# Loading the node features and layer weights of a graph network's first stage from GpSimd instead of SyncE, and turning both weight matrices first

## What is computed

```python
def _L0_gnn_ref(x, Ws_self, Ws_neigh, bs, src, dst):
    deg = segment_sum(ones, dst, n)
    for l in range(3):
        neigh = segment_sum(h[src], dst, n) / clip(deg, 1)
        h = h @ Ws_self[l] + neigh @ Ws_neigh[l] + bs[l]     # relu but for the last
def _mlp(x, W0, b0, W1, b1, g, b):
    return _ln(silu(x @ W0 + b0) @ W1 + b1, g, b)
def _L1_gnn_ref(...):
    e = _mlp(edge_feat, emb_W0, ...)
    e_new = _mlp(concat([e, mesh_nfeat[src], grid_nfeat[dst]]), edge_W0, ...) + e
    agg = segment_sum(e_new, dst, n)
    return _mlp(concat([grid_nfeat, agg]), node_W0, ...) + grid_nfeat
x = _ln(x + _L0_gnn_ref(x, ...)); x = _ln(x + _L1_gnn_ref(x, ...))
```

## Time and profile before

| | us |
|---|---|
| median of 3 runs (2293.87 to 2297.41) | 2294.68 |
| profiled execution | 2294.92 |
| its span from first to last instruction | 2293.2 |
| TensorE busy | 2192.8 |
| VectorE busy | 1502.4 |
| ScalarE busy | 1217.4 |
| GpSimd busy | 1209.9 |

### The profile page before, as it was taken

How to read it: one execution, slowest core, us unless ns; L and a number is a source line. 1 busy time by engine, 2 the same in 40 slices (tenths; PEclk the granted TensorE clock), 3 DMA queues, 4 the chain that set the end, 5 groups by cost and what they waited for, 6 DMA issues and landing times. The chain is left out here.

```text
span 2293.2 us, 44871 instructions
## 1 busy us (share of the span) xinstructions
PE 2192.8 (96%) x13036; PEld 1881.2 (82%) x13040; DVE 1502.4 (66%) x3372; ACT 1217.4 (53%) x2244; POOL 1209.9 (53%) x1721
## 2 busy tenths in 40 slices
PE   2989998999999999999999999999999999999898
PEld 2437886878778989989889898998989989889776
DVE  4813996353846776766766767667676676766666
ACT  1122113242337667666676766676676667667421
POOL 0387107786415555555555555555555555555223
PEclk7999999999999999999999999999999999999899
DMA  8232001010266323333332333333233333333131
GB/s 217 74 78 49 1 0 43 3 44 3 60 199 169 65 61 63 64 59 64 62 65 60 61 65 62 64 64 61 62 59 65 63 64 64 62 59 66 26 95 45
DMA packets 81519, 149.80 MB, mean 65 GB/s; under 512 B 20229, under 2 KB 20695, under 8 KB 81460
## 3 DMA queue, kind: packets, MB, share of 16 engines
q0 software_dynamic: 47248, 93.38, 21.4%
q1 hardware_dynamic: 34212, 55.67, 8.0%
HBM read 128.90 MB, written 19.71 MB: 65 GB/s over the span
## 5 line engine op out<-in xcount | busy, mean ns | idle before, releaser
L1654 ACT ACTIVATE b_bank<-c_bias 128x512 f32<-128x512 f32 x528 | 315.9, 598 | 15.1 <-PE b_bank L1766 5.2
L145 POOL DMA_INDIRECT s_attrs<-k_attrs,k_row_i x170 | 225.4, 1326 | 165.7 <-POOLq L2220 114.9
L1587 DVE CUSTOM_DVE_ANT_0 b_bank<-b_bank,c_p,k_floor 128x512 f32<-128x512 f32 x176 | 132.5, 753 | 255.7 <-PE b_bank L1788 254.8
L1432 POOL DMA_INDIRECT c_from_src<-s_dst_table,c_at_nodes x173 | 278.6, 1610 | 32.0 <-issue 32.0
L1843 PE MATMUL b_bank<-k_m_hi,c_pt_hi 128*128 128x512 f32 x704 | 293.8, 417 | 0.0
L1419 POOL DMA_INDIRECT c_from_src<-s_mesh_table,c_at_nodes x176 | 202.2, 1149 | 152.3 <-POOL c_at_nodes L1415 144.2
L1844 PE MATMUL b_bank<-k_m_lo,c_pt_hi 128*128 128x512 f32 x704 | 277.9, 395 | 0.0
L1845 PE MATMUL b_bank<-k_m_hi,c_pt_lo 128*128 128x512 f32 x704 | 274.0, 389 | 0.0
L1438 POOL TENSOR_TENSOR c_dev<-c_var,k_half 128x1 f32<-128x1 f32 x176 | 99.7, 566 | 327.1 <-DVE c_var L1569 327.1
L1725 ACT ACTIVATE c_h<-c_from_src 128x512 f32<-128x512 f32 x176 | 111.2, 632 | 263.3 <-DVE c_from_src L1608 263.3
L1786 PE MATMUL b_bank<-c_m_hi,c_ht_hi 128*128 128x384 f32 x704 | 222.5, 316 | 6.3 <-DVE c_ht_lo L1574 6.0
(11 more groups left out here) (352 smaller groups left out, 5859.8 us busy)
## 6 DMA issues: line engine op xcount, KB each, us to landing
k_w<-in_L_gnn_Ws_self_dram SPq DMA_DIRECT2D x3, 1024.0 KB, 6.8
k_w<-in_L_gnn_Ws_neigh_dram SPq DMA_DIRECT2D x3, 1024.0 KB, 10.8
c_from_src<-s_mesh_table,c_at_nodes POOLq DMA_INDIRECT x176, 3.5
c_from_src<-s_dst_table,c_at_nodes POOLq DMA_INDIRECT x173, 4.7
s_attrs<-k_attrs,k_row_i POOLq DMA_INDIRECT x170, 2.6
a_mesh<-in_L_gnn_mesh_nfeat_dram SPq DMA_DIRECT2D x10, 224.0 KB
k_h<-in_x_dram SPq DMA_DIRECT2D x1, 2240.0 KB
s_mesh_table<-a_mesh_out SPq DMA_DIRECT2D x10, 224.0 KB
```

The costliest lines, as they stand in the source:

```text
L145: return pool.indirect_dma_start(scratch["attrs"], bass.IndirectOffsetOnAxis(ap=k["row_i"][0:EP, c:c + 1], axis=0), k["attrs"][0:EP, A4 * ...
L1432: pool.indirect_dma_start(from_src[u][:], None, scratch["dst_head" if head else "dst_table"], bass.IndirectOffsetOnAxis(ap=at_nodes[u][:, ...
L1587: dve.tensor_tensor_reduce(var1_bank[:], var1_bank[:], p[u % 2][:], 1.0 / D, k["floor"][:, 0:1], ALU.mult, ALU.add, var[u][:, 0:1]).then_i ...
L1654: act.activation(bank[:], bias[:, m, :], ACT.Copy).then_inc(bank_set, 1)
```

## The change

Four edits, all in `phase_a`. The loads of the node features and of the two weights of the first layer are issued by GpSimd, after its constants and once `weights_in` is 48, and no longer by SyncE. TensorE turns both `w1` before the first product, and ScalarE copies both out first; the bias product stands right after the turning, the totals products after jobs 0 and 1. ScalarE copies the first two turned mesh tiles before, not after, `w_hi` and the first two `hc`.

```diff
@@ SyncE
-        for part in PARTS:
-            sp.dma_start(k["h"][part, :, :], t["x"].rearrange("(b p) d -> p b d", p=NPB)[part, :, :]).then_inc(next_in, 16)
-        sp.dma_start(k["w0"][:], chunked(t["L0_gnn_Ws_self"][0])).then_inc(next_in, 16)
-        sp.dma_start(k["w1"][:], chunked(t["L0_gnn_Ws_neigh"][0])).then_inc(next_in, 16)
-
@@ GpSimd
+        pool.wait_ge(weights_in, 48)
+        for part in PARTS:
+            pool.dma_start(k["h"][part, :, :], t["x"].rearrange("(b p) d -> p b d", p=NPB)[part, :, :]).then_inc(next_in, 16)
+        pool.dma_start(k["w0"][:], chunked(t["L0_gnn_Ws_self"][0])).then_inc(next_in, 16)
+        pool.dma_start(k["w1"][:], chunked(t["L0_gnn_Ws_neigh"][0])).then_inc(next_in, 16)
@@ ScalarE
-        copy_turned(0)
+        for i in range(2):
+            copy_turned(i)
         act.wait_ge(pool_const, 10)
         for j in range(NJ):
-            if j == KC:
-                copy_turned(1)
...
-        act.wait_ge(next_in, MOVED + 32)
-        for i in range(2):
-            act.activation(w_hi[i][:], w[i][:], ACT.Copy).then_inc(w_hi_ok, 1)
-
-        def copy_h(n):
-            if n >= 2:
-                act.wait_ge(hc_turned, n - 1)
-            act.activation(hc[n % 2][:], h[:, n, :], ACT.Copy).then_inc(hc_ok, 1)
-
-        for n in range(2):
-            copy_h(n)
-
...
         for u in range(2):
             mesh_copy(u, u, True)
+        act.wait_ge(next_in, MOVED + 32)
+        for i in range(2):
+            act.activation(w_hi[i][:], w[i][:], ACT.Copy).then_inc(w_hi_ok, 1)
+
+        def copy_h(n):
+            if n >= 2:
+                act.wait_ge(hc_turned, n - 1)
+            act.activation(hc[n % 2][:], h[:, n, :], ACT.Copy).then_inc(hc_ok, 1)
+
+        for n in range(2):
+            copy_h(n)
+
@@ TensorE
-        turn_weight(0)
-        pe.wait_ge(turned_out, KC)
-        jobs(range(KC))
-        turn_weight(1)
+        for i in range(2):
+            turn_weight(i)
         pe.wait_ge(centred, 3)
         pe.matmul(bank[2][:, 0:2], ones[:], bsum[:], start=True, stop=True).then_inc(bias_mm, 1)
+        pe.wait_ge(turned_out, KC)
+        jobs(range(KC // 2))
         pe.wait_ge(totals_ok, 1)
         pe.matmul(earlier_totals, before[0:EP, 0:EP], parts[:], start=True, stop=True)
         pe.matmul(all_totals, ones[0:EP, :], parts[:], start=True, stop=True).then_inc(totals_mm, 1)
+        jobs(range(KC // 2, KC))
         pe.wait_ge(turned_out, 2 * KC)
         jobs(range(KC, 2 * KC))
```

More of the change, by code:

```diff
@@ L659, in _, with mesh_copy @@
             act.activation(rows_out[r % 2][0:m, :], bank[r % 2][0:m, :], ACT.Copy).then_inc(row_out_ok, 1)
+        def mesh_copy(n, u, fixed):
+            if not fixed:
+                act.wait_ge(mesh_mm, n - 1)
+            act.wait_ge(mesh_turned, n + 1)
+            act.activation(mesh_t[u][:, :, 0:NPB],
+                           bank[4 + u][:].rearrange("p (k n) -> p k n", k=KC)[:, :, 0:NPB], ACT.Copy).then_inc(mesh_t_ok, 1)
+        for u in range(2):
+            mesh_copy(u, u, True)
         act.wait_ge(next_in, MOVED + 32)
@@ L671, in _ @@
             copy_h(n)
[L673 to L681, removed]
         with act.Fori(1, NB // 2) as i:
```

## The result

The changed kernel takes **2268.53 us** (median of 4 runs, 2267.89 to 2272.69), the kernel before 2295.97 us beside it (4 runs, 2293.87 to 2297.41): a ratio of 0.9888 with a 95% interval of 0.9876 to 0.99. That is 26 to 27 us faster, inside the predicted range (2256 to 2272) and 8.1 us slower than the forecast of 2260.4. The profiled execution is 2268.53 us with a span of 2266.8, 26.4 us under the span of before.

The account below looks back on a forecast made before the run. Bound: an early TensorE hole, the first store behind SyncE's 4.5 MB of loads. Matrix chain 29.1 + 7.1 = 36.2 us, or 32.5 if gates bind; middle 34.3 off 2294.92 gives 2260.6 (2260.4 against the median); range 2256 to 2272.

Parts of the forecast that it names:

- The hole: TensorE's idle time in the first 57 us, laid to the first store queued behind 4.5 MB of SyncE's loads.
- Sorting chain: Edge sorting on VectorE, then GpSimd's scatters: claimed to start 28.5 us earlier, at L467 by about 27.7.
- The stores: Stores of the squares beside GpSimd's loads: claimed to cost 1.5 us, bounds 0 to 5.
- rival (a): Stores wait behind the loads after all; folds at about 55, matrix chain gains 20 us, time 2275; chance 0.09.
- signs of being wrong: Changed profile: GpSimd's loads ending after 62, store waits of 10 us or more, a_mesh waits, or TensorE awaiting pair read-back.
- The rule on the queues' turns: DMA engines alternate between queues packet by packet, so stores beside the loads lose at most half of the bandwidth.
- The cost of the loads for GpSimd: Issuing four loads on GpSimd: 22 us taken, 29 beside VectorE, free at 54.5, so no cost on the path.
- Rival (b): GpSimd's loads hold it beyond 62.5; 45 us of loads give 2270, far more is slower; chance 0.10, slower 0.03.
- Both weights first: Turning both weights before the products: turns and bias product done at 17.3, folds at 38.8, matrix chain 29.1 us earlier.
- Mesh copies first: First mesh products: TensorE's 4.78 us pause and slow products go, gaining 7.1 us, bounds 4.5 to 7.1.
- Rival (c): The mesh part is empty, as another wait replaces the 4.78 us; matrix chain gains 29.1, time 2266; chance 0.07.
- The gates: Odd gates at the counting, opened behind GpSimd's last scatters: gain 32.5 us if they bind, else 36.2; middle 34.3 taken.

Follow-up runs that it names:

- delayed: The changed kernel, but GpSimd issues its four loads only when all eight squares have been copied: 2264.70 us.
- mesh behind: paced, but SyncE loads the edge attributes and first two mesh tiles behind store 9, no longer ahead of store 0: 2266.65 us.
- no loads: The changed kernel without the four loads of node features and layer weights; GpSimd fills those buffers with a constant instead: 2260.19 us.
- mesh only: The kernel before with only the mesh part: first two turned mesh tiles copied before the high parts of the weights: 2287.28 us.
- paced: The changed kernel with GpSimd's four loads in 18 pieces, two behind each of the product copies 1 to 9: 2260.17 us; again on a third chip: 2266.79 us.

## Why the prediction was right, and where it was wrong

**Right in direction and range, and the chain of reasons held in its main line.** The hole was the first store's, the sort and the matrix products both hung on it (the loads moved alone bring 16.3 us, the other two parts 3.2 and 5.5), and the first stage alone gave the gain: the counting begins 26.3 us earlier (234.2 to 207.91), the span is 26.4 us shorter. Nothing was lost or won behind.

- **Sorting chain**: forecast at L467 by 27.7, measured 28.05 one line later; first scatter 62.5 and 62.69; read-back 174.6 and 175.09. Right within 0.5 us.
- **The stores**: this is the term that failed. Forecast 1.5 us, bounds 0 to 5, from a landing of at most 6 us. TensorE's two waits make 7.9 us, and its squares after them (6.93 and 5.87 us where 5.41 and 3.70 are the durations of the same counts without a pause) 3.7 more: 11.6 in all, and 11.6 - 1.5 is the 10 us by which the folds missed 38.8. Two causes share them. The first pause (2.51 us, and 1.5 for its slow squares) is the first store behind SyncE's own earlier loads, which delayed shows with no load of GpSimd under way and mesh behind takes away; the forecast had the third ScalarE copy near 26.5, it came at 28.39. The second (5.43 and 2.2) is the third store beside GpSimd's loads, which took 12 us. The upper bound was taken from folds and from one landing at a time when no second queue was busy; the text said that no row has a store beside a full second queue, and should have let the bound go up to rival (a), in which the stores wait for all of the loads. That rival, with a chance of 0.09, came half true: 48.75, where the forecast had 38.8 and the rival 55. And the wait of 11.13 us is one of the signs of being wrong that the prediction named itself (a wait for stores of 10 us or more).
- **The rule on the queues' turns.** By the Trainium skill (DMA: Bandwidth & Descriptors, Queues, rings and completion order) a DMA engine takes turns, packet by packet, between the queues that it has work for. From 35 to 41 us the trace agrees, with 239 packets of SyncE and 252 of GpSimd. But SyncE's packets were the smaller ones (0.45 of 1.30 MB), so it got a third of the bytes and not the half that the prediction took for its low end. From 29.1 to 34 us SyncE's queue moved nothing, though the third store had been issued at about 28.9. Whether its packets stood ready at the engines by then, so whether the rule failed or had nothing to act on, no view shows.
- **The cost of the loads for GpSimd**: forecast 22 us, bounds 11 to 29; measured 2.06 + 0.98 + 0.92 = 3.96 us, 1.7 ns a piece. Wrong by a factor of five, but without effect, as the term lay under 34.8 us of waiting. Here the price of an indirect scatter was no guide to that of a direct load. Rival (b) falls with it. (Its sum has a slip: 25.5 + 69 is 94.5, not over 95. And in the earlier trace rows the engines do not move over 200 GB/s all the way to 45 us; five slices from 33 us on stand at 94 to 198. Neither changes the forecast.)
- **Both weights first**: first product at 17.06 (forecast 17.3), first store at 20.56 (near 21). Right.
- **Mesh copies first**: forecast 7.1, measured 7.1 in the kernel that does it alone, and 7.2 in the whole change (from the folds to the counting 159.2 us, 48.75 to 207.91, against 166.3). Rival (c) falls.
- **The gates**: the forecast took the middle of 32.5 and 36.2 as nothing in the rows decided. The trace of before could have decided it: the opener's loop is entered at 219.6, so twelve scatters were waiting. The queue is twelve scatters ahead in before, in the changed kernel (191.7), in no loads, in mesh only and in paced; the gates do not bind, and the full 36.2 was to be had. So 36.2 - 10 is the 26.3 that was measured, and paced on the second chip shows nearly the whole 36.2 at the counting (198.63 against 234.2: 35.6; its span is 34.3 us shorter). The forecast of 34.3 was 1.9 us short there and 10 us long at the stores; the two errors have opposite signs.

The forecast's own range (2257 to 2265), given a chance of 0.72, was missed by 3.5 us. That the wider range held is partly luck: it held because it covered two rivals that did not come true, not because the term that failed had been given its width.

## What to carry to other kernels

A store that an engine waits for is not safe because it has a queue of its own: 4.5 MB issued at once in another queue made one last 12 us, where the first store of mesh behind, issued before any of them, landed in at most 4.2 (copied by 20.35, its buffer free at 24.59). Loads that stand ahead of it in its own queue hold it too. Give out a bulk load in pieces behind the steps that need the stores, and if that is not possible, add a buffer; both together left TensorE no copy to wait for. A queue that runs ahead of its engine is measured where it reaches the next instruction of its list, not where that instruction is released. When no row prices a transfer beside a full second queue, let the range reach to the case in which it gets nothing. And before moving a stage earlier, look at what it will then run beside: the last gains here put the counting beside the scatters, and one chip took 5 to 10 us back there, for a cause that is open.

## What the runs showed of the hardware

- A direct load issued by GpSimd cost it 0.73 and 1.32 us (the two parts of k_h) and 0.98 and 0.92 us (1 MB each), beside VectorE's eight gain steps, 3.85 us for all of them.
- In the changed kernel two indirect scatters beside VectorE's subtractions of w_lo (L572 there, 113.06 to 117.5) took 3.25 and 1.89 us where the others take 1.19:

```profile
113.16 3.25 POOL L391 DMA_INDIRECT s_pairs<-a_sort_pay,a_chunk_row  x1 [0.30 <-issue]
116.71 1.89 POOL L391 DMA_INDIRECT s_pairs<-a_sort_pay,a_chunk_row  x1 [0.30 <-issue]
```

- The same in the other direction: a VectorE instruction on four columns took 3.37 us beside a GpSimd fill (no loads), and 0.17 without one.
- GpSimd's queue ran twelve indirect transfers, 16.5 to 16.9 us, ahead of its engine in before, the changed kernel, no loads, mesh only and paced.
- Two queues with work shared the DMA engines nearly packet for packet (239 and 252 from 35 to 41 us), but a store issued near 28.9 saw its queue move nothing until 34.
- On one chip of three the counting ran at a fifth of its rate beside the scatters (21 matmuls in 6 us for 98), and semaphore instructions of two other queues took up to 0.72 us in place of 0.017. The cause is open.
